# Audio tower on one core: second layer's value products turned, denominators by a running sum, biases in one f16 pass, maxima by DMA, new orders

## The reference, cut to what matters

```
h = tok(x)                                     # conv 5 taps, ReLU, batch norm
h = h + softmax_attention(LN(h))               # 8 heads of 16, band mask in the exponent
h = h + top2_of_8_experts(LN(h))               # 128 -> 256 -> 128, gelu
z = cumsum(K); S = cumsum(K x V)               # second layer, linear attention, 8 heads, values 64 wide
h = h + ((Q S) / max(Q . z, 1e-6)) @ W_out.T
hx = LN(h); y = causal_softmax_attention(hx) @ Wo     # 2 heads of 64
out = h + sum_e softmax(y @ gate)[e] * (gelu(y @ W1[e] + b1[e]) @ W2[e] + b2[e])   # 128 -> 512 -> 128
```

## Time and profile before

| | us |
|---|---|
| three timed runs | 4314.95, 4315.55 (median), 4320.37 |
| profiled execution, first to last instruction (its span) | 4319.1 |
| convolution stage | about 165 |
| a steady round | 125.1 to 126.1 |
| PE busy over the span | 4066.8 (94%) |
| DVE, ACT, POOL busy | 3367.6 (78%), 2784.5 (64%), 2596.6 (60%) |

### The profile page before, as it was taken

How to read it: one execution, slowest core, us unless ns; L and a number is a source line. 1 busy time by engine, 2 the same in 40 slices (tenths; PEclk the granted TensorE clock), 3 DMA queues, 4 the chain that set the end, 5 groups by cost and what they waited for, 6 DMA issues and landing times.

```text
span 4319.1 us, 104773 instructions
## 1 busy us (share of the span) xinstructions
PE 4066.8 (94%) x41344; PEld 3009.8 (70%) x41344; DVE 3367.6 (78%) x8878; ACT 2784.5 (64%) x4796; POOL 2596.6 (60%) x2494
## 2 busy tenths in 40 slices
PE   7678999999999999999999999999999999999998
PEld 3346777777777777777777777777777777777766
DVE  3357888888888888888888888878888887888876
ACT  3235766666676666667666666766666676666654
POOL 2034666666666666666666666666666666666656
PEclk9779999999999999999999999999999999999999
DMA  4200000011100001110000111000101100010000
GB/s 149 68 27 28 18 18 29 28 30 30 30 19 24 22 28 30 30 30 18 23 23 28 30 30 30 23 26 16 30 28 30 30 23 26 16 30 28 28 16 6
DMA packets 136939, 127.62 MB, mean 30 GB/s; under 512 B 28928, under 2 KB 135360, under 8 KB 136448
## 3 DMA queue, kind: packets, MB, share of 16 engines
q1 hardware_dynamic: 136448, 120.91, 9.6%
HBM read 71.05 MB, written 49.55 MB: 28 GB/s over the span
## 4 chain that ended last, share of the span: by engine, by line
PE 56%; DVE 24%; ACT 6%; POOL 5%; issue 4%; DMA 3%; SPq 2%; ACTq 0%; DVEq 0%; POOLq 0%
PE pf L1301 9%; PE pf L1303 8%; PE pf L1302 8%; PE pa L1561 8%; DVE h L1285 4%; PE pa L1447 3%; DVE hid_hi L1266 3%; PE pa L1543 3%; PE pa L1346 2%; PE pa L1433 2%; POOL inv_norm L650 2%; PE pa L1301 2%; ACT xn L726 2%; PE pa L1641 2%; PE pa L1303 2%
## 5 line engine op out<-in xcount | busy, mean ns | idle before, releaser
L660 POOL TENSOR_TENSOR hid_lo<-hid,hid_hi 128x504 f16<-128x504 f32 x1536 | 1835.5, 1212 | 775.8 <-DVE hid_hi L1266 775.8
L886 ACT ACTIVATE hid<-pf,vec 128x504 f32<-128x504 f32 x1536 | 1014.7, 680 | 505.5 <-PE pf L1303 356.9
L1301 PE MATMUL pf<-w_hi,hid_hi 128*126 128x128 f16 x6144 | 1133.7, 224 | 10.7 <-DVE h L1285 10.2
L1303 PE MATMUL pf<-w_hi,hid_lo 128*126 128x128 f16 x6144 | 1115.8, 221 | 0.0
L1302 PE MATMUL pf<-w_lo,hid_hi 128*126 128x128 f16 x6144 | 1115.4, 221 | 0.0
L1301 PEld LDWEIGHTS pf<-w_hi,hid_hi 128*126 128x126 f16 x6144 | 844.1, 137 | 153.5 <-issue 53.2
L1302 PEld LDWEIGHTS pf<-w_lo,hid_hi 128*126 128x126 f16 x6144 | 843.8, 137 | 28.5 <-issue 0.2
L1266 DVE CAST hid_hi<-hid 128x504 f16<-128x504 f32 x1536 | 845.4, 573 | 8.2 <-ACT hid L886 2.7
L1303 PEld LDWEIGHTS pf<-w_hi,hid_lo 128*126 128x126 f16 x6144 | 845.2, 138 | 0.0
L1285 DVE SCALAR_TENSOR_TENSOR h<-pf,gates,h 126x128 f32<-126x128 f32 x2048 | 574.1, 342 | 155.2 <-PE pf L1303 152.6
L616 POOL TENSOR_TENSOR pt<-pt,band 126x262 f32<-126x262 f32 x512 | 351.2, 707 | 527.6 <-ACT pt L773 527.4
(11 more groups left out here) (208 smaller groups left out, 7486.8 us busy)
## 6 DMA issues: line engine op xcount, KB each, us to landing
qk_spread<-terms SPq DMA_DIRECT2D x224, 126.0 KB, 2.5
qk_spread<-terms SPq DMA_DIRECT2D x192, 63.0 KB, 2.3
y_scratch<-hid SPq DMA_DIRECT2D x32, 252.0 KB, 2.1
y_in<-y_scratch SPq DMA_DIRECT2D x32, 252.0 KB, 3.2
terms<-qk_hi SPq DMA_DIRECT2D x32, 252.0 KB, 2.5
terms<-qk_lo SPq DMA_DIRECT2D x32, 252.0 KB, 2.6
qk_spread<-terms SPq DMA_DIRECT2D x32, 252.0 KB
terms<-ot_hi SPq DMA_DIRECT2D x32, 252.0 KB, 2.4
```

What stands on the lines that cost most here:

```text
L660: nc.gpsimd.tensor_tensor(hid_lo[:, c % 8], hid[:, c % HIDS], hid_hi[:, c % 8], ALU.subtract).then_inc(hid_lo_done[c % 2], 1)
L886: nc.scalar.activation(hid[:, c % HIDS], pf[:, c % 2, 0:TOK], func, bias=vec[:, bias:bias + 1]).then_inc(F["hid_ready"], 1)
L1301: nc.tensor.matmul(out, ah, bh, start=start, stop=False, skip_group_check=skip)
L1303: return nc.tensor.matmul(out, al, bh, start=False, stop=stop, skip_group_check=skip)
```

## The change

- **Values of linear attention.** A product now has the values stationary (126 x 64) and 126 score columns moving, and writes 64 output partitions: two heads go to the two column halves of the array, one after the other in the program. Four groups of twelve products stand in place of eight groups of six. The result is already turned, so the four `turn` calls go.
- **Denominators.** DVE forms the running sum of the mapped keys over the tokens (a scan that restarts at the second sequence), multiplies with the queries; PE sums over a head's 16 rows (`head_sum`, four f32 products into four column groups); DVE clips and inverts. SP stores the 8 x 504 reciprocals in DRAM (four DMAs) and loads them back spread over 64 partitions a head (two DMAs, 504 KB each). DVE then multiplies a group at once (four times instead of eight times three instructions).
- **Halves of the linear output.** ACT still makes the high half, now from SBUF; the low half moves from DVE to POOL (four subtractions of 128 x 504 a round).
- **Causal attention.** DVE scales the probabilities by the reciprocal row sums before they are transposed (two reciprocals, eight multiplications); the value product has the values stationary in column halves; the last `turn` and the division go.
- **Biases.** Gates stand three times beside each other, so that one f16 product of 512 columns covers high by high, low by high and high by low; DVE makes the low part (`gate_low`, 32 x 126). `b2` is prepared once, during the convolution stage.
- **Maxima.** The 16 tiles' maxima go into one tile; one f16 product turns it, ACT copies 32 x 126, and SP writes it into the operand rows by two DMAs. The four DVE additions go.
- **Orders.** All strings are new; `l` has 50 steps. The number of activation table loads on ACT in the program falls from 404 to 316.

```diff
-PE_ROUND = ("lhhoalhhaoaoloahlohloaoohlhhlaooahlahohalolhalahllaaoolahollhholallhhalaaolaoloahhaolahhlhoohaoo"
+PE_ROUND = ("hhhhloolaoaholhaqolhohoqllolhahlhohaloahlaoalholahlhqlaoalhalalaaoloalaolaalholhahlahlolaaololhh"
...
+                for _ in range(8):
+                    yield
+                sp.wait_ge(S0["max_copied"], n(p + 1))
+                for r in range(2):
+                    sp.dma_start(q16[0][64 * r + MAX_ROW:64 * r + MAX_ROW + 1].rearrange("o g (t q) -> o (g t) q", t=TILES),
+                                 max_rows[16 * r:16 * r + 16]).then_inc(max_sent, 16)
...
-                    nc.vector.tensor_tensor(q16[0][:, g], pa0[:, g % 3, 0:TOK], q16[0][:, g],
-                                            ALU.add).then_inc(S0["q_shifted"], 1)
...
-                for g in range(GROUPS):
-                    if g >= 3:
-                        pe.wait_ge(S0["q_shifted"], n(p * 4 + g - 2))
-                    for i in range(TILES):
-                        last = nc.tensor.matmul(pa0[:, g % 3, cols(i)], minus_max[0:TILE, i, g],
-                                                ident16[0:TILE, 0:TILE], start=True, stop=True)
-                    last.then_inc(S0["max_turned"], 1)
+                nc.tensor.matmul(pa0[:, 0, 0:TILE], minus_max[0:TILE], ident16[0:TILE, 0:TILE], start=True,
+                                 stop=True).then_inc(S0["max_turned"], 1)
...
+                sp.wait_ge(S1["den_rec"], n(p + 1))
+                for i in range(TILES):
+                    sp.dma_start(rec_dram[:, cols(i)], inv_den[32 * i:32 * i + HEADS]).then_inc(inv_stored, 16)
+                yield
+                sp.wait_ge(inv_stored, n.plain((p + 1) * 16 * TILES))
+                for j in range(2):
+                    src = rec_dram.rearrange("(c j) t -> j c t", j=2)[j]
+                    sp.dma_start(inv_wide[64 * j:64 * j + 64], src.partition_broadcast(64)).then_inc(inv_sent, 16)
...
-                for i in range(TILES):
-                    last = nc.tensor.matmul(pa[a][0:TILE, BIAS2[a], i * D:(i + 1) * D], gate_t[a][:], b2[:, a, i],
-                                            start=True, stop=True)
-                last.then_inc(SS[a]["bias2_ready"], 1)
+                nc.tensor.matmul(pa[a][0:TILE, BIAS2[a]], gate_t[a][0:3 * G_ROWS],
+                                 b2[0:3 * G_ROWS, a].rearrange("p t d -> p (t d)"), start=True,
+                                 stop=True).then_inc(SS[a]["bias2_ready"], 1)
...
+            def gate_low(a, p):
+                dve.wait_ge(SS[a]["gate_t_high"], n(p + 1))
+                part = slice(G_ROWS, 2 * G_ROWS)
+                nc.vector.tensor_tensor(gate_t[a][part], pa[a][part, GATES_T[a], 0:TILE], gate_t[a][part],
+                                        ALU.subtract).then_inc(SS[a]["gate_t_ready"], 1)
...
+                for c in range(CHUNKS):
+                    pool.wait_ge(S1["o1_hi"], n(p * 4 + c + 1))
+                    nc.gpsimd.tensor_tensor(ot_lo[1][:, c % 2], o1[:, c], ot_hi[1][:, c % 2],
+                                            ALU.subtract).then_inc(S1["o1_lo"], 1)
...
+                nc.vector.tensor_tensor_scan(k_sum, restart[:], fs1[:, 1, 0:TOK], 0.0, ALU.mult, ALU.add
+                                             ).then_inc(S1["el_step"], 1)
+                dve.wait_ge(S1["el_step"], n(p * 3 + 3))
+                nc.vector.tensor_tensor(qk_sum, k_sum, fs1[:, 0, 0:TOK], ALU.mult).then_inc(S1["qk_sum_ready"], 1)
+                yield
+                dve.wait_ge(S1["den_ready"], n(p + 1))
+                nc.vector.tensor_scalar(inv_den[:], pa1[:, 1, 0:TILE], 1e-6, None, ALU.max).then_inc(S1["den_done"], 1)
+                dve.wait_ge(S1["den_done"], n(p + 1))
+                nc.vector.reciprocal(inv_den[:], inv_den[:]).then_inc(S1["den_rec"], 1)
...
-                    bank = pa1[0:TILE, 1, 0:4 * (LIN_VALUE + 1)].rearrange("p (h t d) -> p h t d", h=2, t=2)
-                    nc.vector.tensor_scalar(den[0:TILE, g8 % 2].rearrange("p (h t) -> p h t", h=2),
-                                            bank[:, :, :, LIN_VALUE], 1e-6, None, ALU.max).then_inc(S1["den_done"], 1)
-                    dve.wait_ge(S1["den_done"], n(p * 8 + g8 + 1))
-                    nc.vector.reciprocal(inv_den[0:TILE, g8 % 2], den[0:TILE, g8 % 2]).then_inc(S1["den_rec"], 1)
-                    dve.wait_ge(S1["den_rec"], n(p * 8 + g8 + 1))
-                    inv = inv_den[0:TILE, g8 % 2].rearrange("p (h t) -> p h t", h=2).unsqueeze(3).to_broadcast(
-                        [TILE, 2, 2, LIN_VALUE])
-                    dst = o1[0:TILE, 2 * b:2 * b + 2].rearrange("p t (h r) d -> p h t r d", r=2)[
-                        :, 2 * g:2 * g + 2, :, odd]
-                    nc.vector.tensor_tensor(dst, bank[:, :, :, 0:LIN_VALUE], inv, ALU.mult
-                                            ).then_inc(S1["o1_norm"], 1)
...
+                def divide(quad):
+                    b, e = quad // 2, quad % 2
+                    dve.wait_ge(S1["av_done"], n(p * 4 + quad + 1))
+                    tokens = slice(b * SEQ, (b + 1) * SEQ)
+                    nc.vector.tensor_tensor(o1[:, 2 * e:2 * e + 2, tokens],
+                                            pa1[:, 1].rearrange("p (g t) -> p g t", g=2)[:, :, 0:SEQ],
+                                            inv_wide[:, 2 * e:2 * e + 2, tokens], ALU.mult).then_inc(S1["o1_norm"], 1)
...
+                        for t in range(TILES):
+                            last = nc.tensor.matmul(pa1[32 * t:32 * t + 32, 1, 0:TILE], head_sum[:], qk_sum[:, cols(t)],
+                                                    start=True, stop=True, skip_group_check=True)
+                        last.then_inc(S1["den_ready"], 1)
...
+                def values(quad):
+                    b, e = quad // 2, quad % 2
+                    if quad:
+                        pe.wait_ge(S1["o1_norm"], n(p * 4 + quad))
+                    pe.wait_ge(S1["at_ready"], n(p * 8 + 2 * quad + 2))
+                    off = pt[1][0:TILE, 3 * quad % 4]
+                    for g in range(2):
+                        diagonal = pt[1][0:TILE, (3 * quad + 1 + g) % 4]
+                        for qt, kt, factors, blk in ((0, 0, diagonal, 0), (1, 0, off, 2 * g), (1, 1, diagonal, 1)):
+                            for j in range(2):
+                                c = cols(blk + j if factors is off else 2 * j + blk)
+                                first = g * 256 + qt * TILE
+                                last = nc.tensor.matmul(pa1[64 * j:64 * j + 64, 1, first:first + TILE],
+                                                        v1[0:TILE, 2 * b + kt, 4 * e + 2 * g + j], factors[:, c],
+                                                        start=(kt == 0), stop=(kt == qt), skip_group_check=True)
+                    last.then_inc(S1["av_done"], 1)
...
-                        for m in range(2):
-                            hd = 4 * (part - 1) + 2 * m + quad % 2
-                            for qt, terms in ((0, ((0, diagonal, 2 * m),)),
-                                              (1, ((0, off, hd // 2), (1, diagonal, 2 * m + 1)))):
-                                first = (2 * m + qt) * wide
-                                for t, (kt, factors, blk) in enumerate(terms):
-                                    last = nc.tensor.matmul(pa1[0:TILE, 1, first:first + wide], factors[:, cols(blk)],
-                                                            v1[0:TILE, 2 * b + kt, hd], start=(t == 0),
-                                                            stop=(t == len(terms) - 1))
...
-                        turn(1, p * 7 + 1 + c, o1_rows[:, :, c * 128:(c + 1) * 128])
...
+                    pe.wait_ge(S1["o1_lo"], n(p * 4 + c + 1))
...
+                        for kt in range(2):
+                            for hd in range(2):
+                                c0 = 2 * D + hd * HEAD2
+                                last = nc.tensor.matmul(pa1[64 * hd:64 * hd + 64, 1, b * SEQ + kt * TILE:(b + 1) * SEQ],
+                                                        qkv[0:TILE, 2 * b + kt, c0:c0 + HEAD2],
+                                                        fs1[0:TILE, hd, 2 * kt * TILE:(2 + kt) * TILE],
+                                                        start=(kt == 0), stop=(kt == 1), skip_group_check=True)
+                        last.then_inc(S1["pv2_done"], 1)
...
-                        for qt, blocks in ((0, ((0, 0),)), (1, ((0, 1), (1, 2)))):
-                            first = ((2 * b + qt) * HEADS2 + hd) * HEAD2
-                            c0 = 2 * D + hd * HEAD2
-                            for m, (kt, blk) in enumerate(blocks):
-                                last = nc.tensor.matmul(pa1[0:TILE, 1, first:first + HEAD2],
-                                                        fs1[0:TILE, j % 2, cols(blk)],
-                                                        qkv[0:TILE, 2 * b + kt, c0:c0 + HEAD2], start=(m == 0),
```

(6 more changed lines are left out.)

403 lines of the change are left out of this document (214 added, 189 removed).

## The result

The changed kernel is slower: 4504.41 us, median of 4 runs (4491.15 to 4510.96), against 4317.96 for the kernel before (4 runs of the same series). The ratio is 1.0415, 95% interval 1.0388 to 1.0443. The forecast was 4008.

The account below looks back on a forecast made before the run. PE's own work was taken to bound a round: 10.57 us less work minus 1.0 more idle, 9.57 over 32 rounds, is 306 us. With 2 us for the biases, 4319.1 became 4011, median 4008; range 3930 to 4110.

Parts of the forecast that it names:

- rival 1: PE's value, causal and denominator products don't run side by side: 7.3 us a round more, 4241 us; chance 5%.
- rival 2: Each border between column-tiled and full-array PE work drains the array: 48 us more, 4056 us; chance 8%.
- the lowest additions: Lower bound of work added to PE a round, at 0.10 a turn and nothing for entering: 7.0 us, against 8.24 expected.
- I let the idle time of a round grow by 1.0 us: PE's new waits a round: 0.3 us for maxima, 0.4 for reciprocals, 0.3 for the rest.
- I take no change: DVE's busy time a round: 8.8 us lost against rather 8 gained, so still 103 of about 116 us.
- Landing 2.3 as for the smallest spread DMAs: The maxima's DMAs land in 2.3 us, making their path 4.0 us and PE's wait some 0.6 us.
- The reciprocals' 0.4: Idle time allowed a round for the reciprocals' DRAM trip of 10.8 us, just covered by DVE's work ahead: 0.4 us.
- Rival 3: DVE answers later in a shorter round, so PE idles 5 us more instead of 1: 128 more, 4136 us; chance 12%.
- Rival 4: The reciprocals' two loads become the bound; slower from a landing of 15 us, 4412 us at 18; chance 3%.
- PE's idle time passes 6 us a round, or DVE stands still for the two loads: Signs in the changed trace that the prediction is wrong; it expected PE busy near 111 of about 116 us.
- Rival 5: The new orders also remove PE idle time, 1.2 us a round less than now: 70 less, 3938 us; chance 12%.
- The gain at the start and the end: The saving of 9.57 us a round was counted for all 32 rounds, 306 us; 30 rounds would be 287.

Follow-up runs that it names:

- run 4: The changed kernel with the same work but other strings for the five engines' orders in the 30 rounds: 4311.45 us, ratio 0.9995 to the kernel before.
- run 9: The changed kernel with the same work and a second set of the five round orders: 4185.0 us, ratio 0.969 to the kernel before.
- run 2: The changed kernel without the two 504 KB reciprocal loads and DVE's wait for them, a constant multiplied instead: 4368.04 us, ratio 1.0133.
- run 3: The changed kernel with GpSimd's squares moved one place later, behind a low half of the experts: 4506.98 us, ratio 1.0451.

## Why the prediction was wrong

**Right: what the change does to PE's work.** A value group was forecast at 1.43 us from its start to the next. The changed kernel's PE timeline:

```profile
1623.53 1.51 PE L1613 MATMUL pa<-pt,v 126*64 126x126 f32 x24
1624.97 0.43 PE L1496 MATMUL pa<-qk_spread 64*126 64x252 f16 x4
```

1.44 us: the halves run side by side, and rival 1 falls. The turned maxima are one product with 0.06 us to the next start. The table loads fall by 88. PE busy was forecast at 121.5 - 10.57 = 110.9 us a round; it is 117.3 in the change, and with the passes of the low stretches counted at full clock 113.1 there, 114.5 in run 4 and 112.1 in run 9. The 1.2 to 3.6 us that are left I did not split further; rival 2's borders can be part of them. One bound of the prediction's sum is added up wrongly: the lowest additions come to 6.9 us, not 7.0; nothing rests on it.

**The step that failed: "I let the idle time of a round grow by 1.0 us … between -1.2 … and +5".** It grew by 14.91 - 4.05 = 10.9. The overrun of a round, 132.2 - 116.0 = 16.2 us, is 9.9 of idle time over the 5.05 forecast, 4.2 of the lower clock in PE's busy time, and 2.1 of PE work. Of the 10.9, the waits on DVE make 8.2 and those on DMAs 3.2; waits on ACT fell by 1.6, and the rest grew by 1.1. The sum priced three things wrongly:

- *"I take no change" for DVE.* The sum counted instructions by their mean durations of before. A mean in the earlier trace rows already held a part of waiting for GpSimd's port (the cast: 573 ns there, of casts at 412 alone and 661 beside GpSimd; 487 in run 9), and where new orders put the gates' chain beside the squares and low halves, it grew. DVE rose to 107.5 us a round with the same work for which run 9 needs 96.9. The scan is 1.20 us, within its bounds. The rule that speaks of it stands in the Trainium skill (above) and was not weighed. How much of the 8.2 us is this and how much the longer chain through DVE is not shown: run 9 still waits 5.1 us a round on DVE.
- *"Landing 2.3 as for the smallest spread DMAs".* It is 5.5, because the loads are under way; from the turned product to the scores it is 6.7 us in the median, not 4.0. The prediction said that the maxima "can be late with" the loads, but gave that no price on PE. Taking the loads away gave 136 us (run 2).
- *The reciprocals' 0.4.* The trip takes 10.0 us, near the 10.8 forecast, but the sum let it begin when the reciprocals are ready. It begins 2.3 us later, behind other issues in SP's string, and DVE stands 2.5 us a round for it (81.2 / 32).

**Not in the sum at all: the clock.** The waits of some 3 us end in a stretch at 1.2 GHz. The forecast had priced a wait by its length. In the change this costs about 4.2 us a round, two fifths of what the idle time grew by.

**Rivals.** Rival 3 (idle time takes part of the gain, 4136) had the direction of the idle time and, for DVE, the place; but at +10.9 instead of +5 with the clock on top it ended on the other side. Rival 4 (reciprocals the bound) comes in small as DVE's waits for `inv_wide`:

```profile
DVE o L1232 <- DMA inv_wide<-reciprocals: 81.2, 32, 3.6
```

The prediction's own condition for being wrong, "PE's idle time passes 6 us a round, or DVE stands still for the two loads", came true in both parts. Rival 5 (orders that take idle time away) came with no set of orders for the changed work; the lowest idles 8.80.

**The gain at the start and the end** is not settled. Outside the 27 rounds the change takes 4501.2 - 3569.9 = 931.3 us, and before 4319.1 - 3390.2 = 928.9. But three of these five rounds run the same strings as the 27; at each kernel's own pace they explain 20 us more, and what is left would be 18 us shorter than before. With the rounds cut at another instruction (the scaling of the next pair) it comes out 2 us longer.

That GpSimd's instructions hold VectorE's and that the loads hold the maxima is shown by runs 3 and 2; that the loss lay in the orders is shown by runs 4 and 9 together: same work, other orders, 193 and 319 us less. How the 319 us divide between port, loads, clock and short waits is not measured apart, and for the port alone no run shows a gain in time, as run 3 only moved the wait. Whether the forecast's 116 us a round can be reached with any orders stays open: run 9 is 5.6 above it.

## What to carry to other kernels

When a change lightens the bounding engine but comes with new orders, price the order too: for each step on the chain ask what runs on the engine that shares its ports, which big transfer is under way and what stands ahead in the issuing engine's string, not only how long the step took before. A small DMA that a chain waits for belongs clear of large loads in time; another queue did not save it here. And price a wait of some 3 us on TensorE above its length: two of them a round, 5.96 us, cost 4.2 us more in slow passes.
